# Moving one softplus behind four gelus: ScalarE's order in slot 14 of a fused Mamba, expert and attention kernel

## What is computed

```python
xb = silu(conv(x_br)); Bm = xb @ W_b; Cm = xb @ W_c
delta = softplus(xb @ W_delta + b_delta)
h = exp(delta * A) * h + delta * Bm * xb      # over time, 16 states per channel
y = sum(h * Cm over the states) + xb * Dp
x = layernorm(x + (y * silu(z)) @ W_out + residual)
...
for e in range(4):                            # the experts
    h = gelu(xi @ We1[e] + be1[e])
    out += (h @ We2[e] + be2[e]) * combine_w[e]
```

## Time and profile before

| | |
|---|---|
| median of 3 runs | 3641.55 us |
| the profiled execution | 3645.86 us |
| its span, first to last instruction | 3644.1 us |
| TensorE busy | 3312.8 us (91%) |
| VectorE busy | 2839.1 us (78%) |
| ScalarE busy | 2176.2 us (60%) |
| GpSimd busy | 1527.7 us (42%) |
| mean granted TensorE clock | 0.963 |

### The profile page before, as it was taken

How to read it: one execution, slowest core, us unless ns; L and a number is a source line. 1 busy time by engine, 2 the same in 40 slices (tenths; PEclk the granted TensorE clock), 3 DMA queues, 4 the chain that set the end, 5 groups by cost and what they waited for, 6 DMA issues and landing times. The chain is left out here.

```text
span 3644.1 us, 41261 instructions
## 1 busy us (share of the span) xinstructions
PE 3312.8 (91%) x14448; PEld 1552.3 (43%) x14448; DVE 2839.1 (78%) x3484; ACT 2176.2 (60%) x3604; POOL 1527.7 (42%) x1294
## 2 busy tenths in 40 slices
PE   4239999999999999989889999999999999998998
PEld 2025556555655555555522222322222222222666
DVE  5898899999989899974468888888888888882444
ACT  5355666656565756532157777777777777777221
POOL 2998899999999999971010000000000000000110
PEclk8679999999999999999999999999999999999999
DMA  3111223131222212232020000000000000000010
GB/s 109 32 38 52 73 70 102 63 112 64 94 84 82 87 62 93 73 121 85 26 97 19 19 19 19 19 17 17 15 17 19 19 19 19 19 10 7 23 35 29
DMA packets 108187, 180.19 MB, mean 49 GB/s; under 512 B 13989, under 2 KB 81689, under 8 KB 99417
## 3 DMA queue, kind: packets, MB, share of 16 engines
q1 hardware_dynamic: 107992, 177.72, 15.5%
HBM read 151.58 MB, written 26.08 MB: 49 GB/s over the span
## 5 line engine op out<-in xcount | busy, mean ns | idle before, releaser
L1927 DVE TENSOR_REDUCE tile_max<-ps 128x1 f32<-128x1024 f32 x976 | 1149.9, 1220 | 248.2 <-PE ps L1723 248.2
L1866 ACT ACTIVATE probs<-ps 128x512 f32<-128x512 f32 x2048 | 1106.4, 598 | 375.4 <-PE ps L1736 373.8
L1486 POOL TENSOR_TENSOR vals<-vals,c_sb 128x512 f32<-128x512 f32 x512 | 681.5, 1363 | 131.9 <-DVE state L1278 111.0
L1273 DVE TENSOR_TENSOR_SCAN vals<-stacks,state,ps 128x512 f32<-128x512 f32 x512 | 655.0, 1279 | 103.0 <-POOL heads_v L1497 38.1
L1736 PE MATMUL ps<-stacks 101*128 101x512 bf16 x2048 | 701.8, 382 | 24.7 <-PEq L245 12.2
L1497 POOL TENSOR_TENSOR heads_v<-heads_v,vals 128x512 f32<-128x512 f32 x512 | 648.0, 1298 | 8.7 <-issue 0.2
L1723 PE MATMUL ps<-stacks 99*128 99x512 bf16 x1952 | 583.8, 380 | 0.0
L227 POOL COPY heads_v<-vals 128x256 f32<-128x256 f32 x32 | 12.7, 402 | 1344.7 <-PE ps L1746 1322.2
L1746 PE MATMUL ps<-probs,heads_v 128*32 128x512 f32 x4096 | 545.3, 605 | 0.0
L731 PE MATMUL ps<-x1T,e_w 128*128 128x512 f32 x1024 | 464.1, 599 | 26.2 <-ACT hid L1041 26.2
L1736 PEld LDWEIGHTS ps<-stacks 101*128 101x128 bf16 x2048 | 195.7, 96 | 658.9 <-ACT probs L1866 423.2
(11 more groups left out here) (201 smaller groups left out, 3055.1 us busy)
## 6 DMA issues: line engine op xcount, KB each, us to landing
e_w<-in_e_w SPq DMA_DIRECT2D x64, 1024.0 KB, 7.1
c_sb<-scratch_c SPq DMA_DIRECT2D x128, 256.0 KB, 3.4
stacks<-scratch_q SPq DMA_DIRECT2D x192, 64.0 KB
stacks<-scratch_k SPq DMA_DIRECT2D x192, 64.0 KB
scratch_q<-parts SPq DMA_DIRECT2D x16, 384.0 KB, 4.2
scratch_k<-parts SPq DMA_DIRECT2D x16, 384.0 KB, 4.4
xr<-scratch_x SPq DMA_DIRECT2D x10, 512.0 KB, 4.4
xn_tok<-in_x SPq DMA_DIRECT2D x8, 512.0 KB, 4.9
```

What stands on the lines that cost most here:

```text
L1273: v.tensor_tensor_scan(h[:, n % 2, m, :], decay[:, n % 2, m, :], ps[:, 0, :], state[:, n, m:m + 1], ALU.mult, ALU.add).then_inc(s["h_ready ...
L1486: last = nc.gpsimd.tensor_tensor(h[:, n % 2, m, :], h[:, n % 2, m, :], c_sb[:, n % C_RING, :], ALU.mult)
L1866: fn(probs[:, step % 2, qc, :], ps[:, S_BANK[i], :], ACT.Exp)\
L1927: v.tensor_reduce(tile_max[:, t, half:half + 1], ps[:, at:at + PAIR, :].rearrange("p a n -> p (a n)"), AX.X, ALU.max).then_inc(s["max_read ...
```

## The change

In slot 14 ScalarE runs the four gelus of the fourth expert's first half (ups) before soft_exp and soft_log of delta's second half, instead of after them. On VectorE, deltas(f, 1) moves from the end of slot 14 to slot 15, behind base and before blocks 2 and 3 of the scan. No arithmetic changes.

```diff
--- before.py
+++ after.py
@@ -1160,13 +1160,13 @@
                         copy_delta(f, 3)
                     if n == 1 and first(i):
                         norm0(1)
-                    if n == 14 and inside(f):
-                        soft_exp(f, 1)
-                        soft_log(f, 1)
                     if inside(m):
                         for j in range(2 * NE):
                             if n == SLOT_OF_UP[j]:
                                 ups(m, j // 2, j % 2)
+                    if n == 14 and inside(f):
+                        soft_exp(f, 1)
+                        soft_log(f, 1)
                     if n in DECAYS_LAST and inside(i):
                         decays(i, n + 1)
                     if n == 7 and inside(m):
@@ -1420,6 +1420,8 @@
                                 down(m, j // 2, j % 2)
                         if n == 15:
                             base(m)
+                    if n == 15 and inside(f):
+                        deltas(f, 1)
 
                     if inside(i):
                         for blk in range(2, DB):
@@ -1451,8 +1453,6 @@
                         split_bc(f)
                     if n == 14 and inside(m):
                         down(m, 2, 1)
-                    if n == 14 and inside(f):
-                        deltas(f, 1)
                     for _ in range(START.get((i, n), 0) if isinstance(i, int) else 0):
                         start_head(begun[0])
                         begun[0] += 1
```

## The result

| | before | after |
|---|---|---|
| median, 5 runs each | 3642.84 us | 3661.69 us |
| lowest to highest | 3640.53 to 3644.67 | 3659.66 to 3662.58 |
| span of the profiled execution | 3644.1 us | 3660.8 us |
| mean granted TensorE clock | 0.963 | 0.959 |

The changed kernel is slower by 18.85 us; the ratio is 1.0052, with a 95% interval from 1.0037 to 1.0067. Slower was the likeliest case of the prediction, but 3661.7 us lies above its range of 3642.5 to 3658, and the 18.85 us are 1.75 times the 10.8 us of its sum. The median before is of five runs here and 1.29 us above the median of three from which the prediction counted.

A forecast was written before the change was run, and what follows sets the result against it. Three engines were all but full and the loop closed through gated, where GpSimd would come last; 1.25 us for its later end plus 0.55 us for meeting times_c, in six iterations, gave +10.8 us: 3652.4 us, range 3642.5 to 3658 us.

The forecast's parts named there:

- When the softplus is ready: ScalarE, slot 14: Ln ends 12.6 us after T (start of the fourth expert's first matmuls), softplus 7.6 us later than before.
- rival C: ScalarE: each of two added table switches costs another 1.28 us, +15.4 us on top, 3667.8 us; chance 0.03.
- When VectorE wants it: VectorE, slot 15: it stands before deltas at T+9.5 and waits 3.2 us for the softplus.
- GpSimd ends last before gated, and gated meets its next step: Slot 15 into slot 0: gated waits for GpSimd, +1.25 us, then runs against GpSimd's states, +0.55 us, per iteration.
- Rival A: VectorE's new wait is only traded for old ones and GpSimd doesn't bind: +1 to +3 us, 3643.5 us; chance 0.22.
- rival B: TensorE's gain in slot 14 sets the pace and gated moves forward: 8.4 us less, 3633.1 us; chance 0.10.
- It buys nothing: TensorE waits for gated the longer: TensorE ends the half about 1.4 us earlier, then waits 3 us for gated instead of 0.27; priced at nothing.

The follow-up runs named there:

- e4: Changed kernel with deltas of the second half moved behind the last scan and the reduction of slot 15: 3640.63 us, kernel before 3643.28 us.
- e5: Changed kernel with the softplus behind the first two of the four gelus instead of behind all four: 3642.79 us, kernel before 3642.32 us.
- e1: Changed kernel with ten added matmuls on TensorE ahead of its wait for gated in iterations 2 to 7: 3658.5 us, kernel before 3643.28 us.
- e9: The kernel of e1 (ten added matmuls in the changed kernel) run again beside the changed kernel: 3657.46 us, changed kernel 3662.17 us.
- e3: Kernel before with VectorE's part alone, deltas in slot 15 behind base, ScalarE's order as before: 3654.27 us, kernel before 3643.28 us.
- e11: The kernel of e4 (changed kernel, deltas behind slot 15's last scan) timed once more: 3640.31 us, ratio 0.9992.
- e2: Kernel before with ScalarE's part alone, gelus first, deltas left at the end of slot 14: 3688.77 us, kernel before 3643.28 us.

## Why the prediction was wrong

- **When the softplus is ready**, T+12.6: right within 0.1 us. Switches cost 1.30 us, the added ones too (end of the fourth gelu 1223.01 to start of Exp 1224.32, and end of Exp 1225.38 to start of Ln 1226.68). The drain of 1.38 us that the Trainium skill (ScalarE: Activation LUTs, What ACT_TABLE_LOAD costs) counts with each was not there; rival C is out.
- **When VectorE wants it**, T+9.5 and a wait of 3.2 us: the wait was 2.53 us and VectorE came at T+10.1. It ended slot 14 later from T than before, and the sum had taken that from the old timeline. It changed nothing further on, because the Ln was last either way.
- **GpSimd ends last before gated, and gated meets its next step**: right, with gated waiting 0.60 us for line 1497 and taking 3.33 us. Per iteration 1.5 us for 1.8. The stretch gave 8.2 us for 10.8. Rival A, that the new wait is only traded, falls with this; rival B, faster, was the true outcome from T to gated only where VectorE no longer waited for the Ln (e4 and e5, both T+28.1), and even there not in the runs.
- **The step that failed** is "It buys nothing: TensorE waits for gated the longer". The wait was foreseen at 3 us and measured at 2.6 to 3.4 us, and priced at nothing. In three of six iterations line 675 behind it ran 2.9 us longer at a granted clock of 0.71: 8.6 us in each of two profiles, and nothing once the wait was filled (e1, e9). The Trainium skill (TensorE: Matmul & The Clock Gate, Part 1) says that the array's clock is set by how busy it has lately been, between two levels; the rows above agree, with the clock low behind some of the long waits and behind none of the filled ones. The missing term would have been 2.9 us for each iteration in which it falls. With none to six of them that is 0 to 17 us, and the range would have had to reach to about 3675 us.
- How the 18.85 us are made up: about 8 us are the later gated, which the sum had at 10.8. The clock in line 675 takes 8.6 us, of which iteration 7 alone gives back 3.0; filling the wait was worth 3 to 5 us in the runs, and that is its price net. Some 6 us are left, about what the other versions show too, and their cause is open. The stretches put 2.8 us of them between project_z and project_bc, where two profiles of one kernel differ by 2 to 4 us themselves. The time lies 3.7 us above the range, and with the wait filled the kernel took 3658.5 and 3657.5 us, right at its upper bound. So the clock's term is about what took it out of the range, and the open part is the rest of the way from the 3652.4 us of the sum.

The trace of the kernel before had a sign of the missing term, in slot 1 of iterations 1 and 8. The same 32 matmuls took 8.6 and 8.9 us there, at a granted clock of 0.83 and 0.81:

```profile
244.86 8.61 PE L675 MATMUL ps<-w_out,gate 128*128 128x256 f32 x32 [10.82 <-DVE gate L1288]
...
1619.41 8.86 PE L675 MATMUL ps<-w_out,gate 128*128 128x256 f32 x32 [1.93 <-DVE gate L1288]
```

## What to carry to other kernels

What a late input costs depends on how much of its reader's work stands behind the waiting instruction: the same late softplus cost 45 us with all of a slot behind it, 19 us with half, and nothing with none. Work that doesn't need the input goes first. When an edit makes TensorE wait some 3 us in a place where it waited 0.3, add a second price for the clock to the range, and look in the trace before for places where the same line already ran slower behind a wait. And where several engines are all but full, moving an instruction to where it is free to start can cost too: in e3 VectorE lost a wait of 0.98 us and found 2.10 us of other waits and 0.9 us of a slower instruction. And a gain read off one stretch of a trace (e4 and e5, 8 to 9 us) is not yet a gain of the kernel.

## What the hardware showed that was not expected

- TensorE's granted clock fell behind waits of 2.83 to 3.43 us before line 675 in three of six iterations, in 2, 4 and 6 never, though the waits there were 2.63 to 3.28 us. In the kernel before it fell behind 1.93 us, in iteration 8. The length of the wait alone doesn't tell which. With ten matmuls of 0.22 us in it, it fell in none of twelve.
- In the router's stretch the granted clock was 0.91 in most iterations of the kernel before and 0.83 in most of e4 and e11, with the same matmuls: 9.0 us won between project_bc and project_out in e4 gave 2.7 us in the runs.
- Line 1254 (128x1024, both operands in SBUF) took 1.22 us in e4, where GpSimd stood idle as it began, and 2.29 us in e2, where it began in the midst of GpSimd's instructions; the longest in these profiles is 2.38 us. gated took 3.33 us where it began 0.07 us behind a GpSimd instruction (changed kernel), and 2.88 us where it began 0.54 us behind one (kernel before).
